# Who squares and who evacuates in the statistics pass of a cross attention: GpSimd takes three of eight squares, ScalarE five, VectorE the next layer's projections

## The reference

```python
qk = jnp.einsum('bhqd,bhkd->bhqk', Q, K)          # 16 heads, 256 x 4096
scores = qk / math.sqrt(dk)
max_sim = scores.max(axis=-1).mean(axis=-1)
probs = jax.nn.softmax(scores, axis=-1)
entropy_proxy = jnp.var(probs, axis=-1, ddof=1).mean(axis=-1)   # needs sum(exp) and sum(exp^2)
...                                               # a small network gives t for each head
attn = jax.nn.softmax(qk / (2.0 * t), axis=-1)
out = jnp.einsum('bhqk,bhkd->bhqd', attn, V)
```

## Time and profile before

| | us |
|---|---|
| median of 3 runs | 1445.9 (1439.41 to 1446.11) |
| the profiled execution, its own time | 1446.76 |
| its span, first to last instruction | 1445.0 |
| the first pass, about 52.0 to 311.5 | 259.5 |

### The profile page before, as it was taken

One profiled execution on the slowest core, in us unless ns is written; L12 is line 12 of the kernel. 1 busy time (PEld: TensorE's weight loads), 2 busy tenths in 40 slices (PEclk: granted clock), 3 DMA queues, 4 the chain that ended last, 5 costly groups with the idle time before them and its releaser, 6 DMA issues. The chain is left out here.

```text
span 1445.0 us, 25386 instructions
## 1 busy us (share of the span) xinstructions
PE 1151.4 (80%) x8423; PEld 697.4 (48%) x8423; DVE 837.7 (58%) x1556; ACT 918.7 (64%) x1240; POOL 443.0 (31%) x149
## 2 busy tenths in 40 slices
PE   7687777747999869899958787778778778866798
PEld 3333433423344346678833444444444444444687
DVE  5798988870011266452226777777777766845312
ACT  3699999976998625433324777777777777634210
POOL 1000000000000004000005888888888887920000
PEclk9899999987999868989976999999999999977899
DMA  7864445437554070034458888887888888715040
GB/s 258 261 187 119 116 113 129 108 85 148 105 112 88 22 238 0 1 97 151 151 201 300 286 293 283 304 295 269 289 293 289 297 296 288 244 52 176 16 159 8
DMA packets 97047, 257.50 MB, mean 178 GB/s; under 512 B 11193, under 2 KB 41305, under 8 KB 85466
## 3 DMA queue, kind: packets, MB, share of 16 engines
q1 hardware_dynamic: 96992, 256.79, 57.5%
HBM read 165.31 MB, written 91.92 MB: 178 GB/s over the span
## 5 line engine op out<-in xcount | busy, mean ns | idle before, releaser
L1874 POOL TENSOR_TENSOR xb_row<-xb_row,w_mask 128x1024 f32<-128x1024 f32 x128 | 418.5, 3281 | 297.1 <-DVE xb_row L1904 296.7
L1904 DVE TENSOR_TENSOR xb_row<-xb_cont_ps,xb_row 128x1024 f32<-128x1024 f32 x128 | 156.7, 1224 | 112.1 <-PE xb_cont_ps L1706 111.4
L1832 ACT COPY xb_turned<-xb_turn_ps 128x1024 f32<-128x1024 f32 x128 | 129.5, 1012 | 81.9 <-PE xb_turn_ps L1744 81.2
L1744 PE MATMUL xb_turn_ps<-_ident,xb_row 128*128 128x128 f32 x1024 | 147.3, 290 | 37.5 <-ACT xb_row L1826 28.3
L1368 POOL TENSOR_TENSOR b_tc<-b_raw,w_waves 128x512 f32<-128x512 f32 x4 | 5.1, 1266 | 534.9 <-ACT b_raw L1354 534.9
L1744 PEld LDWEIGHTS xb_turn_ps<-_ident,xb_row 128*128 128x128 f32 x1024 | 119.2, 149 | 98.5 <-issue 63.9
L1915 DVE CUSTOM_DVE_ANT_0 xb_row<-xb_row,xb_minus 128x1024 f32<-128x1024 f32 x128 | 165.6, 1294 | 0.0
L1706 PE MATMUL xb_cont_ps<-xb_kk,xb_qq 32*128 32x512 f32 x528 | 163.7, 699 | 1.4 <-DVE xb_out L1896 1.4
L567 DVE TENSOR_REDUCE xa_stats<-xa_b_ps 128x1 f32<-128x1024 f32 x128 | 153.1, 1219 | 9.4 <-PE xa_b_ps L466 9.3
L828 ACT ACTIVATE xa_probs<-xa_psT,xa_t_now 128x1024 f32<-128x1024 f32 x128 | 141.1, 1113 | 25.1 <-PE xa_psT L787 25.0
L1706 PE MATMUL xb_rel_ps<-xb_kk,xb_qq 32*128 32x512 f32 x496 | 152.6, 693 | 4.5 <-ACT xb_out L1821 3.2
(11 more groups left out here) (362 smaller groups left out, 1756.6 us busy)
## 6 DMA issues: line engine op xcount, KB each, us to landing
xb_row<-rel_scores SPq DMA_DIRECT2D x128, 512.0 KB, 5.5
rel_scores<-xb_out SPq DMA_DIRECT2D x32, 1024.5 KB, 5.3
rel_scores<-xb_out SPq DMA_DIRECT2D x32, 1024.0 KB, 4.9
b_e_w<-in_L_ffn_e_w SPq DMA_DIRECT2D x32, 513.0 KB, 3.5
w_w<-in_L_ffn_w SPq DMA_DIRECT2D x24, 512.0 KB, 4.6
xa_k<-first_parts SPq DMA_DIRECT2D x24, 384.0 KB, 5.0
value_rows<-xa_values SPq DMA_DIRECT2D x16, 544.0 KB, 6.1
xb_kk<-key_blocks SPq DMA_DIRECT2D x17, 512.0 KB, 8.0
```

Source lines behind the costliest of these rows:

```text
L1744: mm = nc.tensor.transpose(turn_ps[:, k * P:(k + 1) * P], row[:, u, at:at + P], f.ident[:])
L1832: nc.scalar.copy(turned[:, part].rearrange("p k n -> p (k n)"), turn_ps[:]).then_inc(turned_sb[part], 1)
L1874: nc.gpsimd.tensor_tensor(row[:, u, at:at + SUB], row[:, u, at:at + SUB], mask[:, t, half * HALF + at:half * HALF + at + SUB], ALU.mult).t ...
L1904: nc.vector.tensor_tensor(row[:, u, at:at + SUB], cont_ps[:], row[:, u, at:at + SUB], ALU.add).then_inc(s["cont_out"], 1)
```

## The change

All of it is in the first pass. Of a head's eight quarters, ScalarE squares five (0, 2, 3, 5, 6) and GpSimd three (1, 4, 7). GpSimd has no sum alongside: it squares into `rest` (128 x 1024), adds the upper half onto the lower twice (512 and 256 columns), and leaves 256 partial sums for each of its quarters in `folded`. VectorE no longer squares. It sums a head's three folded quarters in one reduction (`unfold`) just ahead of `keep`, which is now a reduction over a dimension of one, and it takes over `product_out`: product j-1 stands where square 2j-1 stood, between the two minima of j. ScalarE's own squares all go to one buffer, so that each waits for the one before.

```diff
-            squares = f.sb(inner, "squares", [P, 2, QUARTER])
+            squares = f.sb(inner, "squares", [P, QUARTER])
+            ACT_SQUARES, POOL_SQUARES = (0, 2, 3, 5, 6), (1, 4, 7)
+            FOLDS, FOLDED = 2, QUARTER // 4
+            folded = f.sb(inner, "folded", [P, 2, NG_SQ, FOLDED])
...
@@ ScalarE
-                    act.wait_ge(s["odd_squared" if u % 2 else "even_squared"], NU // 2 * h + u // 2 + 1)
+                    before, used = (h, u - 4) if u >= 4 else (h - 1, u + 4)
+                    if used in POOL_SQUARES:
+                        act.wait_ge(s["pool_product"], (FOLDS + 1) * (NG_SQ * (before + 1) + POOL_SQUARES.index(used)) + 1)
+                    else:
+                        act.wait_ge(s["act_squared"], NA * (before + 1) + ACT_SQUARES.index(used) + 1)
...
                             exponential(it, c, 2 * j)
                             exponential(it, c, 2 * j + 1)
-                            square(it, c, 2 * j)
-                            product_out(it, c, j)
+                            for u in (2 * j - 1, 2 * j):
+                                if u in ACT_SQUARES:
+                                    square(it, c, u)
...
@@ VectorE
+                def product_out(it, c, j):
+                    dve.wait_ge(s["projected"], NU // 2 * h + j + 1)
...
+                        nc.vector.tensor_scalar(whole[:, c % 2, j * BANK:(j + 1) * BANK], src,
+                                                bcol[:, 1 + c // KC, c % KC:c % KC + 1], None, ALU.add
+                                                ).then_inc(s["product_out"], 1)
...
+                        nc.vector.tensor_copy(dst, src.rearrange("p (k h d) -> p h k d", k=half, h=H // 2)
+                                              ).then_inc(s["product_out"], 1)
...
+                def unfold(it, c):
+                    dve.wait_ge(s["pool_folded"], NG_SQ * (h + 1))
+                    nc.vector.tensor_reduce(stats[:, c % 2, 2, 1:NU:3], folded[:, c % 2], AX, ALU.add
+                                            ).then_inc(s["unfolded"], 1)
...
                             minimum(it, c, 2 * j)
                             if j > 0:
-                                square(it, c, 2 * j - 1)
+                                product_out(it, c, j - 1)
...
                             minimum(it, c, 2 * j + 1)
                             if j == 1 and c > 0:
+                                unfold(it, c - 1)
                                 keep(it, c - 1)
...
+            @block.gpsimd
...
+                    pool.wait_ge(s["exp_done"], NU * (h + 1) + u + 1)
+                    pool.wait_ge(s["pool_product"], done)
...
+                    nc.gpsimd.tensor_tensor(rest[:], exps[:, u % 4], exps[:, u % 4], ALU.mult).then_inc(s["pool_product"], 1)
+                    width = QUARTER
+                    for k in range(FOLDS):
+                        width //= 2
+                        pool.wait_ge(s["pool_product"], done + k + 1)
+                        out = rest[:, 0:width] if k < FOLDS - 1 else folded[:, c % 2, n]
+                        ins = nc.gpsimd.tensor_tensor(out, rest[:, 0:width], rest[:, width:2 * width], ALU.add)
```

More of the change, by code:

```diff
@@ L568, in minimum @@
                                             ).then_inc(s["min_ready"], 1)
-                def square(it, c, u):
-                    h = HPB * it + c
-                    dve.wait_ge(s["exp_done"], NU * (h + 1) + u + 1)
-                    dve.wait_ge(s["odd_squared"], NU // 2 * h + u // 2 + 2)
-                    dve.sem_inc(s["squares_begun"], 1)
-                    nc.vector.tensor_tensor_reduce(out=squares[:, 1], in0=exps[:, u % 4], in1=exps[:, u % 4], scale=1.0,
-                                                   scalar=0.0, op0=ALU.mult, op1=ALU.add,
-                                                   accum_out=stats[:, c % 2, 2, u:u + 1]).then_inc(s["odd_squared"], 1)
+                def product_out(it, c, j):
+                    h, slot = HPB * it + c, 3 * j + 2
+                    dve.wait_ge(s["projected"], NU // 2 * h + j + 1)
+                    src = ps[:, slot % 4, 0:BANK]
+                    if j < 2:
+                        if j == 0:
+                            dve.wait_ge(keys_stored[c % 2], KEYS_OUT * (it * HPB // 2 + c // 2 + 1))
+                        nc.vector.tensor_scalar(whole[:, c % 2, j * BANK:(j + 1) * BANK], src,
+                                                bcol[:, 1 + c // KC, c % KC:c % KC + 1], None, ALU.add
+                                                ).then_inc(s["product_out"], 1)
+                    else:
+                        if j == 2:
+                            if c < 2:
+                                dve.wait_ge(s["ones_set"], 1)
+                            dve.wait_ge(values_stored[c % 2], 16 * (it * HPB // 2 + c // 2 + 1))
+                        half = CPH // 2
+                        dst = values[:, c % 2, :, (j - 2) * half:(j - 1) * half, 0:DK]
+                        nc.vector.tensor_copy(dst, src.rearrange("p (k h d) -> p h k d", k=half, h=H // 2)
+                                              ).then_inc(s["product_out"], 1)
@@ L593, in body @@
                             if j > 0:
-                                square(it, c, 2 * j - 1)
+                                product_out(it, c, j - 1)
                             elif c > 0:
-                                square(it, c - 1, NU - 1)
+                                product_out(it, c - 1, NU // 2 - 1)
                             elif not first:
-                                square(it - 1, HPB - 1, NU - 1)
+                                product_out(it - 1, HPB - 1, NU // 2 - 1)
@@ L599, in body @@
                             minimum(it, c, 2 * j + 1)
                             if j == 1 and c > 0:
+                                unfold(it, c - 1)
                                 keep(it, c - 1)
                             elif j == 1 and not first:
+                                unfold(it - 1, HPB - 1)
                                 keep(it - 1, HPB - 1)
                 bodies(dve, body)
-                square(NB - 1, HPB - 1, NU - 1)
+                product_out(NB - 1, HPB - 1, NU // 2 - 1)
@@ L607, in _, with square @@
+                unfold(NB - 1, HPB - 1)
                 keep(NB - 1, HPB - 1)
                 dve.wait_ge(s["kept"], H + 2)
+            @block.gpsimd
+            def _(pool):
+                pool.sem_inc(s["pool_product"], (FOLDS + 1) * NG_SQ)
+                def square(it, c, u):
+                    h, n = HPB * it + c, POOL_SQUARES.index(u)
+                    done = (FOLDS + 1) * (NG_SQ * (h + 1) + n)
+                    pool.wait_ge(s["exp_done"], NU * (h + 1) + u + 1)
+                    pool.wait_ge(s["pool_product"], done)
+                    if n == 0:
+                        pool.wait_ge(s["kept"], h + 1)
+                    nc.gpsimd.tensor_tensor(rest[:], exps[:, u % 4], exps[:, u % 4], ALU.mult).then_inc(s["pool_product"], 1)
[5 more added lines that the diff above has]
+                        ins = nc.gpsimd.tensor_tensor(out, rest[:, 0:width], rest[:, width:2 * width], ALU.add)
+                        ins.then_inc(s["pool_product"], 1)
+                        if k == FOLDS - 1:
+                            pool.wait_ge(s["pool_product"], done + k + 2)
+                            pool.sem_inc(s["pool_folded"], 1)
+                with pool.Fori(0, NB) as it:
+                    for c in range(HPB):
+                        for u in POOL_SQUARES:
+                            square(it, c, u)
```

44 lines of the change are left out of this document (13 added, 31 removed).

## The result

The changed kernel takes 1421.95 us (median of 4 runs, 1420.97 to 1425.9) where the kernel before takes 1443.57 (4 runs, 1439.41 to 1446.11): ratio 0.9858, 95% interval 0.9824 to 0.9892. That is faster, and by more than my range allowed (1424 to 1446, likeliest 1433.0). In the 68 later runs of the kernel before its times lay between 1433.4 and 1454.0; this spread turns out to belong to the case.

What follows compares the result with a forecast made beforehand. Two chains within 0.1 to 0.2 us bound the first pass: VectorE's square chain and ScalarE's own work. Heads of 14.65 instead of 15.54 us give -14.2 over 16, the end +1.3: -12.9, so 1433.0, range 1424 to 1446.

Steps and rivals of the forecast that it cites:

- The bound: First pass, steady head: VectorE's square chain sets 15.5 us, with ScalarE's own 3.71 to 3.81 per 3.88 us turn close behind.
- ScalarE and VectorE after the change: First pass: ScalarE's 14.00 us a head plus 0.25 and 0.40 of waits gives 14.65; VectorE's sum is 13.3.
- the wait of square 6: ScalarE, first pass: square 6 shares square 5's buffer and waits until it is complete, +0.25 us a head.
- exponential 5: ScalarE, first pass: held up by the 6.9 us chain through TensorE and VectorE, about 0.4 us late in each head.
- GpSimd: First pass: product taken at 2.34 us, not 3.28; 4.57 us a quarter, 13.7 a head of 14.6, so hidden.
- The first heads "stay as they are": Start of the first pass: these heads wait for transfers and TensorE's clock in either kernel, so no change in time.
- The end: End of the first pass: next block 7.6 us behind the last exponential instead of 5.15, costing +1.3 us, between 0 and 2.5.
- The sum's last step: Everything outside the first pass and its end: nothing else is touched, so the total changes by -12.9 us only.
- GpSimd as the bound: Rival, first pass: GpSimd's product takes 3.28 us, a head 16.5, total 1464 us; chance 0.09.
- the 5.18 given: First pass: GpSimd's time per quarter, in us, at which the change turns from gain to loss (15.54 / 3).
- TensorE's chain: Rival, first pass: TensorE's chain takes the place of VectorE's square, no change in time, 1439 to 1446 us; chance 0.14.
- ScalarE alone at 14.0: Rival, first pass: waits of square 6 and exponential 5 vanish, heads 14.0 to 14.1 us, total 1422; chance 0.15.

Runs made afterwards that it cites:

- e8: Kernel before, with ScalarE's copies of the products out of PSUM left out: 1441.2 us in one run, steady heads of 15.54 us.
- e7: Kernel before, with VectorE's four squares a head replaced by one-column copies: 1428.1 us in one run, steady heads of 14.96 to 14.97 us.
- e11: Changed kernel, with GpSimd multiplying the exponentials by a context tile instead of by themselves: 1425.1 us in one run, product 2.353 us.
- e12: Changed kernel, with VectorE's copy of product j-1 behind both minima of j instead of between them: 1447.3 us in one run, steady heads of 15.39 us.
- e1: Changed kernel run again with no edit: 1421.8 us (6 runs), ratio 0.9851 to the kernel before.
- e2: Kernel before, with the first head's loads of the second pass moved behind the store and load of the maxima on SyncE's queue: ratio 1.0001.
- e14: Changed kernel, with four extra matmuls in TensorE's idle gap at each head of the second layer's cross attention: 1417.99 us, ratio 0.9811 to the kernel before.
- e13: Kernel before, with four extra matmuls in TensorE's idle gap at each head of the second layer's cross attention: 1435.22 us, ratio 0.9944.
- e9: Changed kernel, with one more GpSimd addition of 512 columns behind each of its squares: 1468.9 us in one run, heads 17.3 us in the mean.

## Why the prediction missed, point by point

- **The bound.** Right, and shown from both sides: VectorE's chain sets 15.54 (e8 leaves it and stays there), ScalarE's sum comes next at 14.96 (e7).
- **ScalarE and VectorE after the change.** Right within 0.16 us a head: 14.65 forecast, 14.49 measured. Of the terms, the wait of square 6 was 0.14 and not 0.25, and an exponential takes 1.09 and not 1.10; exponential 5 came 0.41 late, as worked out.
- **GpSimd.** Right that it is hidden, and right that L1915's form goes with the 3.28: of the 49 instances of L1874 that the timeline of the kernel before shows singly, 47 start while L1915 runs and take 3.25 to 3.36, and the two that don't take 2.34. Nothing in the new stage had that effect (1.892 to 1.894 in 48 instances, 2.345 to 2.363 in e11). The Trainium skill's page "SBUF — State Buffer", in "SBUF: two separate sides", blocks GpSimd only for a VectorE instruction in a two-port mode or with two SBUF inputs, and these traces agree. The value itself was a third one, since one tile on both sides is faster than two. I had named this as what could be wrong. For the time it was worth nothing, as GpSimd is not the bound.
- **The first heads "stay as they are".** Wrong by 1.3 us in head 0 (19.47 against 18.19): VectorE now does the copy that waits for SyncE's first counters, and minimum 3 waits behind it (idle 2.17 us at 59.65, exponential 3 idle 2.63); e12, where the minimum stands ahead of the copy, has a head 0 of 15.4. Head 0 itself varies, 16.6 to 18.2 in four profiles of the old first pass and 17.6 to 19.5 in seven of the new one, partly with its clock (19.47 at 0.81 in the profile after, 17.74 at 1.00 in e1). And the other three heads that begin an iteration gained 0.6 together instead of 2.7: before they took 15.38 at a clock of 1.00 and 16.61 twice at 0.90, after 15.65 to 16.28 at 0.89 to 0.90. So the pass gave -11.9 and not -14.2.
- **The end.** The step that VectorE comes later was right (7.24 against 7.6). That this costs 1.3, and at best nothing, was wrong: it gave 2.2. I had looked at SyncE only as an engine that is busy, and not at what its loads do to the store behind them (5.88 us from store to load, 1.47 in e2 without them).
- **The sum's last step failed.** "Nothing else is touched" held for the instructions, and I took it for the time. 9.4 us came from a stage 440 us further on, where TensorE's clock fell behind 3 gaps instead of 10, and 1.7 from the stages between. The sum had put this term at nothing without a reason. The trace of before had the sign in it: 34 us of idle time before one line in that stage, with the four matmuls behind it at 1.13 and at 2.05, and runs that differ by 6.7 us. Without this term the change is worth 14 us in the first two profiles, and 13 to 17 in e14 against e13; on the medians of before (1443.6 to 1446.7) that would have been a time of about 1427 to 1434, inside the range.
- **The rivals.** GpSimd as the bound: did not happen, and e9 shows it at 5.47 a quarter, above the 5.18 given. TensorE's chain: did not happen, and e12 shows that a copy 1.2 us later would have brought it. ScalarE alone at 14.0: the time came out at this rival's 1422, but not by its mechanism, since the waits that it wanted gone are there.

## What to carry to other kernels

Where the chains through two engines are both within 4% of a turn's length, name the chain that passes through each and ask whether the change shortens both; either half alone gave 0.57 and 0 us a head here, the whole gave 1.05. A copy that frees a buffer belongs where its consumer waits for it, not behind work of the same engine that has time.

An untouched stage is not an unchanged time. If a later stage lets TensorE idle for 2 us in each head and the kernel's runs spread, a shift ahead of it can come with a gain or loss of the size of the change itself (9 us here beside 14); fill such gaps first (four matmuls without use gave the kernel before 7 us in the median, and a spread of 10 us instead of 20), and then compare versions.

## What the runs showed of the hardware

- GpSimd's elementwise product of 128 x 1024 float32 took 1.892 us with one tile on both sides and 2.353 with two tiles (48 instances each, the same stage). With two tiles it took 2.34 or, begun while VectorE was in an instruction with two operands in SBUF, 3.25 to 3.36.
- TensorE's granted clock behind the same idle gap of 2.3 us was 1.00 in some heads and 0.5 in others of one execution, and each fall made the half of a head around it 1.4 to 1.8 us longer in the kernel before. With about 2.0 of the 2.3 us filled by matmuls it stayed at 1.00 in all 14 heads of the middle of the stage (e13, e14).
- A store of 24 KB and the load that waits for it were 5.88 us apart with 1 MB of loads issued just in front in the same queue, and 1.47 us with these behind.
